# First layer's cross attention as one program instead of a loop of stages

## What is computed

```
xn = layernorm(ctx, ln_x_g, ln_x_b)          # 120 rows of 96
ln = layernorm(x, ln_l_g, ln_l_b)            # 128 rows of 128
q  = ln @ Wq.T
kv = concatenate([xn @ Wkv.T, ln @ Wlkv.T])  # keys: context rows and the rows themselves
k, v = split(kv); split_heads(q, k, v)       # 2 heads of 64
qn = rmsnorm(q) * 64 ** -0.5
kn = rmsnorm(k)
attn = where(mask, qn @ kn.T, -max)          # the mask hides context rows only
out  = softmax(attn) @ v
x = layernorm(x + out @ Wo.T + bo)
```

## Time and profile before

| | us |
|---|---|
| median of 3 runs | 6116.07 |
| the profiled execution | 6122.38 |
| its span, first to last instruction | 6120.6 |
| PE busy in the span | 4768.7 (78%) |
| DVE busy | 4188.5 (68%) |
| ACT busy | 2855.4 (47%) |
| POOL busy | 2427.0 (40%) |
| granted PE clock, mean | 0.877 of 2.4 GHz |

### The profile page before, as it was taken

The page is one execution under the profiler, slowest core; times in us unless marked ns, Lnnn a source line. Parts: engine busy times, 40 slices in busy tenths (PEclk is TensorE's granted clock), DMA queues, the critical chain, the costliest instruction groups (busy, mean ns, idle before and its releaser), DMA issues. The chain is left out here.

```text
span 6120.6 us, 86534 instructions
## 1 busy us (share of the span) xinstructions
PE 4768.7 (78%) x29231; PEld 2856.0 (47%) x29232; DVE 4188.5 (68%) x8013; ACT 2855.4 (47%) x4726; POOL 2427.0 (40%) x2136
## 2 busy tenths in 40 slices
PE   8655999999999999777746676665887689835667
PEld 5543566666666666424522222222664354314444
DVE  3323888888888889576376999997553336547545
ACT  2211677777777777463224554542333325423211
POOL 0011767667677677342174666664001201000100
PEclk9755999999999999887768999998998769966788
DMA  0000000000000000000000000000000000002000
GB/s 14 5 0 30 5 1 20 1 20 1 5 17 1 20 1 5 4 1 2 4 0 7 0 0 0 0 0 12 0 0 13 10 7 7 1 11 58 6 22 7
DMA packets 74599, 49.57 MB, mean 8 GB/s; under 512 B 27801, under 2 KB 68780, under 8 KB 73452
## 3 DMA queue, kind: packets, MB, share of 16 engines
q1 hardware_dynamic: 72171, 43.64, 2.8%
q0 software_dynamic: 2048, 1.05, 0.1%
...
## 5 line engine op out<-in xcount | busy, mean ns | idle before, releaser
L3199 POOL TENSOR_TENSOR l_attn_read<-l_attn_state,l_attn_c_rows 128x1024 f32<-128x1024 f32 x256 | 603.6, 2358 | 329.9 <-DVE l_attn_state L3102 329.0
L2076 POOL TENSOR_TENSOR l_ffn_t<-l_ffn_t 128x512 f32<-128x512 f32 x384 | 488.2, 1271 | 523.1 <-DVE l_ffn_t L1943 523.1
L3102 DVE TENSOR_TENSOR_SCAN l_attn_state<-l_attn_decay,psum 128x1024 f32<-128x1024 f32 x256 | 584.9, 2285 | 8.1
L1676 PE MATMUL psum<-l_ffn_wq,l_ffn_xsT 128*128 128x512 f32 x1152 | 564.9, 599 | 20.8 <-DVE l_ffn_t L1943 12.0
L2904 PE MATMUL psum<-l_attn_read,ident 128*128 128x512 f32 x1024 | 496.9, 608 | 5.4 <-DVE l_attn_yz L3110 3.0
L2895 PE MATMUL psum<-l_attn_parts,pick 96*128 96x512 bf16 x512 | 200.6, 395 | 307.6 <-DVE psum L3094 307.5
L2087 POOL TENSOR_TENSOR l_ffn_p<-l_ffn_p,l_ffn_sm 128x512 f32<-128x512 f32 x384 | 399.2, 1040 | 61.8 <-DVE l_ffn_sm L1975 45.4
L2082 POOL TENSOR_TENSOR l_ffn_t<-l_ffn_t,l_ffn_ss 128x512 f32<-128x512 f32 x384 | 400.4, 1043 | 0.7 <-DVE l_ffn_ss L1958 0.7
L203 POOL TENSOR_SCALAR rstd<-mean_var 128x4 f32<-128x4 f32 (+1 forms) x24 | 5.5, 230 | 979.2 <-DVE mean_var L192 979.2
L3021 ACT COPY l_attn_c_rows<-psum 128x512 f32<-128x512 f32 x256 | 149.6, 584 | 468.4 <-PE psum L2895 468.3
L3094 DVE TENSOR_TENSOR psum<-psum,l_attn_du 128x1024 f32<-128x1024 f32 x256 | 315.6, 1233 | 32.1 <-POOL l_attn_du L3176 4.6
...
## 6 DMA issues: line engine op xcount, KB each, us to landing
...
```

The source lines that it names most:

```text
L1676: nc.tensor.matmul(ring[it % 2], xsT[:, n % 2, m % G, :], wq[:, z, i * 512:(i + 1) * 512], start=True, stop=True).then_inc(itemed, 1)
L2076: nc.gpsimd.tensor_tensor(t1[:, m % G, i, :], t1[:, m % G, i, :], t2[:, x % 3, :], ALU.add).then_inc(added, 1)
L3102: nc.vector.tensor_tensor_scan(state[:, k % 3, :], decay[:, k % 3, :, :, :].rearrange("p h g t -> p (h g t)"), drive, 0.0, ALU.mult, ALU.a ...
L3199: nc.gpsimd.tensor_tensor(read[:, k % 3, :].rearrange("p (h n) -> p h n", h=2), state[:, k % 3, :].rearrange("p (h n) -> p h n", h=2), row ...
```

## The change

`l0_xattn` is written anew; nothing else differs. The loop of stages becomes one `stage` with 48 semaphores and a program written out for six steps `t = 0..5`. In step t the engines work on three groups at once: group `a = t` is normed, projected and scaled (A), group `b_ = t - 1` is attended to (B), and group `f = t - 2` gets its residual and layer norm (F). Step 0 holds only A, step 1 A and B, steps 2 and 3 all three, step 4 B and F, step 5 F.

What is computed in another way:

- The scores are made twice. Once as before, rows of queries (`lat_score`, `ctx_score`), from which DVE takes only the maximum of each query and head. Then turned, rows of keys (`lat_turned`, `ctx_turned`), into which PE first brings minus the maximum, and the mask, by a product with `select` or `select_mask` (two rows in each half of `top_turned`: the maximum, and ones). ACT exponentiates them from PSUM, so the probabilities need no transposition.
- The two heads lie in the two halves of the partitions (`half(z)`), so a product of one head uses 64 rows of the array, or writes 64 of its columns (`value`).
- The sums of the probabilities are products with 64 columns of ones (line 973, 975), which leaves them repeated over the partitions: DVE takes the reciprocal of all 128 x 512 numbers (1156) and multiplies once (1161). The result is already turned for the output projection.
- The output bias is added to the residual on POOL (1201) instead of by PE. POOL also scales the normed context (1182) and the final rows (1190); ACT scales the normed rows of x (1048). All were DVE's.
- The mask's load is issued first, the bias is loaded repeated over 128 partitions.

```diff
--- before.py
+++ after.py
@@ -808,119 +808,397 @@
...
+        bo, x_bias = sb("bo", [128, D]), sb("x_bias", [128, G, D])
...
+        select, select_mask = sb("select", [128, T]), sb("select_mask", [128, NB, NC_])
+        ones64 = sb("ones64", [128, dh])
...
+        half = lambda z: slice(64 * z, 64 * z + 64)
+        A = lambda t: t if t < NG else None
+        B = lambda t: t - 1 if 0 <= t - 1 < NG else None
+        F = lambda t: t - 2 if 0 <= t - 2 < NG else None
+        STEPS = range(NG + 2)
...
+                def qk_turn(g):
+                    for part, m in enumerate(parts):
+                        pe.wait_ge(normed, 3 * g + part + 1)
+                        if g and part == 0:
+                            pe.wait_ge(ctx_exp, H * g)
+                            pe.wait_ge(o_ready, g)
+                        for b in range(G):
+                            last = nc.tensor.transpose(K.bank[4 + part][:, b * m:(b + 1) * m], qkn[:m, part, b * D:(b + 1) * D], K.ident[:m, :m])
...
+                def lat_score(g):
+                    pe.wait_ge(qk_moved, 3 * g + 2)
+                    for b in range(G):
+                        at = slice(b * T, b * T + T)
+                        for z in range(H):
+                            last = nc.tensor.matmul(K.bank[4 + z][:, at], qT[half(z), at], kT[half(z), at], start=True, stop=True)
+                            if b == G - 1:
...
+                    for z in range(H):
+                        nc.tensor.matmul(K.bank[6 + z][:, :KEYS], K.ones[64 * z:64 * z + 1, :], mask_all[64 * z:64 * z + 1, g * G:(g + 1) * G, :], start=True, stop=False,
...
+                def turn_top(g):
+                    pe.wait_ge(top_ready, g + 1)
+                    for b in range(G):
+                        last = nc.tensor.transpose(K.bank[4][:, b * T:(b + 1) * T], top[:, b, :], K.ident[:])
...
+                def lat_turned(g):
+                    pe.wait_ge(top_moved, g + 1)
+                    for z in range(H):
+                        nc.tensor.matmul(K.bank[5 + z], select[half(z), :], top_turned[half(z), :], start=True, stop=False, skip_group_check=True)
+                    for b in range(G):
+                        at = slice(b * T, b * T + T)
+                        for z in range(H):
+                            last = nc.tensor.matmul(K.bank[5 + z][:, at], kT[half(z), at], qT[half(z), at], start=False, stop=True, skip_group_check=True)
+                            if b == G - 1:
+                                last.then_inc(lat_low, 1)
+
...
+                def ctx_turned(g):
+                    for z in range(H):
+                        for b in range(G):
+                            nc.tensor.matmul(K.bank[(7, 4)[z]][:NC_, b * T:b * T + T], select_mask[half(z), g * G + b, :], top_turned[half(z), b * T:b * T + T],
+                                             start=True, stop=False, skip_group_check=True)
+                            last = nc.tensor.matmul(K.bank[(7, 4)[z]][:NC_, b * T:b * T + T], cT[half(z), b * NC_:(b + 1) * NC_], qT[half(z), b * T:b * T + T],
+                                                    start=False, stop=True, skip_group_check=True)
+                        last.then_inc(ctx_low, 1)
...
+                    for z in range(H):
+                        nc.tensor.matmul(K.bank[5][half(z), :], ones64[:], p_lat[:, z, :], start=True, stop=False, skip_group_check=True)
+                    for z in range(H):
+                        last = nc.tensor.matmul(K.bank[5][half(z), :], ones64[:NC_, :], p_ctx[:, z, :], start=False, stop=True, skip_group_check=True)
+                    last.then_inc(summed, 1)
...
+                            nc.tensor.matmul(K.bank[6][half(z), at], v_lat[:, g % 2, b, dh * z:dh * z + dh], p_lat[:, z, at], start=True, stop=False, skip_group_check=True)
...
+                for t in STEPS:
+                    a, b_ = A(t), B(t)
+                    if b_ is not None:
+                        qk_turn(b_)
+                    if a is not None:
+                        in_turn(a, False)
+                    if b_ is not None:
+                        lat_score(b_)
+                    if a is not None:
+                        in_turn(a, True)
+                    if b_ is not None:
+                        ctx_score(b_)
+                    if a is not None:
+                        project(a, 0)
+                        project(a, 1)
+                    if b_ is not None:
+                        turn_top(b_)
+                    if a is not None:
+                        project(a, 2)
+                    if b_ is not None:
+                        lat_turned(b_)
+                    if a is not None:
+                        values_in(a, False)
+                    if b_ is not None:
+                        ctx_turned(b_)
+                    if a is not None:
+                        values_in(a, True)
+                    if b_ is not None:
+                        value(b_)
+                        out(b_)
...
+                const(nc.vector.tensor_tensor(first[:], K.ident[:, 0:1], K.ident[:, 64:65], ALU.add))
+                const(nc.vector.tensor_tensor(second[:], K.ident[:, 1:2], K.ident[:, 65:66], ALU.add))
+                const(nc.vector.tensor_scalar(first[:], first[:], -1.0, None, ALU.mult))
+                const(nc.vector.tensor_scalar(select[:], K.ones[:], first[:], None, ALU.mult))
...
+                        nc.vector.tensor_tensor(K.y[:].rearrange("p g d -> p (g d)"), K.bank[7], x_bias[:].rearrange("p g d -> p (g d)"), ALU.add).then_inc(y_made, 1)
...
+                    if a is not None and a:
+                        stats_of(a)
...
+                        nc.vector.tensor_tensor(top[:].rearrange("p g (z r) -> p g z r", z=H)[:, :, :, 0], top_l[:], top_c[:], ALU.max).then_inc(top_ready, 1)
...
+                            dve.wait_ge(ctx_low, H * b_)
+                        nc.vector.tensor_copy(top_turned[:], K.bank[4]).then_inc(top_moved, 1)
...
+                        dve.wait_ge(summed, 2 * b_ + 1)
+                        nc.vector.reciprocal(inv[:], K.bank[5]).then_inc(recip, 1)
+                        dve.wait_ge(recip, b_ + 1)
+                        dve.wait_ge(summed, 2 * b_ + 2)
+                        if b_:
+                            dve.wait_ge(out_dot, b_)
+                        nc.vector.tensor_tensor(oT[:], K.bank[6], inv[:], ALU.mult).then_inc(o_ready, 1)
...
+                        for i in range(G):
+                            nc.gpsimd.tensor_scalar(cn[:, i, :], K.ctx_all[:, a * G + i, :], rs_x[:NC_, 1, i:i + 1], nb_x[:NC_, 1, i:i + 1], ALU.mult, ALU.add).then_inc(c_normed, 1)
...
+                            ins = nc.gpsimd.tensor_scalar(K.x_all[:, f * G + i, :], K.y[:, i, :], rs[:, i:i + 1], nb[:, i:i + 1], ALU.mult, ALU.add)
...
+                        nc.gpsimd.tensor_tensor(x_bias[:], K.x_all[:, b_ * G:(b_ + 1) * G, :], rows(bo[:], G), ALU.add).then_inc(x_biased, 1)
```

361 lines of the change are left out of this document (261 added, 100 removed).

## The result

| | before | after |
|---|---|---|
| median, us | 6116.15 (4 runs, 6109.86 to 6118.06) | 5966.89 (4 runs, 5963.5 to 5968.24) |
| profiled execution / span | 6122.38 / 6120.6 | 5968.24 / 5966.5 |
| first attention, to its last write | 258.49 | 253.08 |
| the stage | 329.9 | 174.0 |
| all behind it | 5532.2 | 5539.4 |

The ratio is 0.9757 (0.974 to 0.9774): 149.3 us faster between the medians, where 162.1 were forecast. The time lies inside the predicted range, 13 us above the predicted one.

A forecast was written before the change was run, and what follows sets the result against it. The stage was taken as bound by a serial chain. Steps of 28 + 35 + 72 + 22 + 6.5 = 163.5 us, with borders 167.8 instead of 329.9, gave -162.1: 5954.0 us, range 5926 to 6000.

The forecast's parts named there:

- step 0: Stage opening, from first transfer issue through group 0's norms, projections and scaling until L913 may go: 28 us.
- step 4: Step without projections, attention of the last group, counted to its output projection: 22 us.
- last L989 to last write: Step 5, the last group's output 1.1, residual and statistics 2.1, POOL power 1.7 and four rows: 6.5 us.
- the changes: PE empties itself when switching between full and half array, six or seven times a step: 1.3 us in all.
- the tail: End of a step: DVE's reciprocal with the scaling sticks out beyond PE's values by 2.6 us.
- the clock term: PE's clock falls in each gap, returns after some 8 us of mixed products: 40 passes slower, +4.1 us a step.
- the part that I took as zero: Layers behind the stage: same work, their clock may fall otherwise by a few us, counted as zero.
- 1 (the clock never recovers): Rival: half-array products too thin to raise PE's clock in the stage; +44 us, 5998 us; chance 0.09.
- 2 (never falls): Rival: PE's idle gap counts less than thought, clock stays up; -16 us, 5938 us; chance 0.07.
- 3 (pairs don't overlap): Rival: alternating half-array products don't overlap or half wait for loads; +31 to +60 us, about 6000; chance 0.07.
- 4 (the written-out list is fetched too slowly): Rival: late code holds PE at each instruction; at 0.11 us each the kernel takes 6130 us; chance 0.02.
- 5: Rival: A and B run one after the other, projections waiting too; +15 us, 5969; chance 0.74 together with the forecast.

The follow-up runs named there:

- e_sems: Changed kernel with 48 more unused semaphores, so the stage's border clears 96 instead of 48; 5965.08 us (one run).
- e_again: The changed kernel measured once more with no edit; 5960.12 us, ratio 0.973.
- e_early: Changed kernel with each next group's norms (DVE statistics, POOL's and ACT's part) made one step earlier; 5935.69 us, ratio 0.9696.
- e_fill: Changed kernel with 26 useless identity products on PE ahead of its wait before L879 of groups 1 to 3; 5948.44 us, ratio 0.9722.
- e_ctxpairs: Changed kernel with the turned context scores issued with the two heads alternating instead of head by head; 5951.03 us, ratio 0.9721.
- e_copy: Changed kernel with DVE's reciprocal of the sums replaced by a copy, so it computes something else; 5949.54 us, ratio 0.9712.
- e_serial: Changed kernel with PE doing all of group a's turnings and projections before group b's scores, not interleaved; 5985.45 us (one run).
- e_best: e_early plus alternating context heads, group 0's norms ahead of the parameter wait, output projection behind the next group's turnings; 5926.99 us, ratio 0.9674.
- e_all: e_best with next group's statistics and POOL norms earlier still, and DVE's mask conversion after POOL scales its statistics; 5919.86 us, ratio 0.9679.

## Why the prediction was right

**The mechanism.** The stage was priced as a serial chain, whole, at 167.8 us; it took 174.0. Stretch by stretch:

| | predicted | measured |
|---|---|---|
| opening border and step 0, to the first L913 | 1.75 + 28 | 30.2 |
| step 1, to the first L989 | 35 | 34.9 |
| steps 2 and 3 | 36, 36 | 36.96, 35.99 |
| step 4 | 22 | 24.2 |
| last L989 to last write | 6.5 | 8.0 |
| closing border | 2.5 | 3.71 |

Inside step 2: L989 to L879 10.2 predicted, 9.7 measured; the products to L950 some 12 (6.5 + 4.1 and waits) and 13.7; the rest 10.6 and its share of the changes, 11.1; the tail 2.6 and 2.4. The power of 8 columns was interpolated at 1.7 and took 1.67; the reciprocal, extrapolated from 1 and 64 columns to 512, at 3.4 (the two rows give 3.3) and took 3.36. ACT's and POOL's four rows took 1.65. These were among the widest bounds of the prediction, and its values were right.

**Where the sum was lucky.** The terms of step 0 add up to 29.5 and the hand-overs, not to the 28 that the prediction states. The 28 held (28.4 from the first issue at 254.83 to L913 at 283.24) because the second move lay under the first projections: turning and moving took 2.9 us ahead of them (269.09 to 271.94), not 4.2. And the clock term was right in its price (4.1) with a length that was too short; see below.

**What was off, 6.2 us.** Step 4 (+2.2). Its terms leave out the output projection with which a step begins, 8 passes, 1.6 us (391.12 to 392.75), and the wait for the maxima was 1.6 instead of 1. In this step the clock was low twice. The first time was in the sum (35 passes at "4 to 7", taken as 6, and 5.95 measured), the second was not: the products of L950 and L954 took 3.5 us (401.70 to 405.19), in step 2 at 2.4 GHz 1.95. Even so, all from L950 to the end of the values took 11.2 us, against 8.8 + 0.7 + 1.3 in the sum, so the passes there had been priced 1.1 us too high. The windows of the changed kernel in step 4:

```profile
391.40:394.80 3.40, 3.40 (x18) 3.40 (x18) 1.74 (x8) 0.79 (x2) 0.00 (x0) 0.50 0.00 0
394.80:401.70 6.90, 4.33 (x44) 2.86 (x42) 3.58 (x10) 1.14 (x2) 4.67 (x9) 0.99 0.01 2
401.70:405.10 3.40, 3.40 (x20) 2.37 (x21) 0.00 (x0) 0.00 (x0) 0.00 (x0) 0.50 0.00 0
```

The last group (+1.5): the last projection ran at 1.2 GHz, 2.1 us instead of 1.1, and POOL's rows took 0.44 each instead of 0.372. The border (+1.2): I set 2.5 for 48 semaphores without a row to stand on; e_sems gives 0.055 each, and by that 0.84 + 44 x 0.055 = 3.3 of the 3.7 is explained.

**The rest of the difference, 149.3 instead of 162.1.** 6.2 of 12.8 are the stage. 1.8 are the part that I took as zero: -5.4 ahead of the stage and +7.2 behind it. 4.8 are the choice of execution: the profiled one of before lay 6.2 above its median, that of after 1.4. Of the 7.2 us, 5.7 came in one place, whose window stands here for before and for after: the same instructions, 123.20 us at a mean clock of 0.92 and 128.90 at 0.86.

```profile
2881.00:3004.20 123.20, 109.44 (x1379) 84.69 (x1380) 55.33 (x126) 48.41 (x93) 7.12 (x19) 0.92 0.02 5
```

```profile
2718.60:2847.50 128.90, 115.36 (x1377) 89.44 (x1378) 55.43 (x126) 48.60 (x93) 7.15 (x19) 0.86 0.02 5
```

In e_again the same layers took the same 5539.4, in the other kernels up to 12.7 less and 5.5 more; what sets it was not settled.

**The clock.** Predicted: it falls in each gap before L879 and comes back after some 8 us of mixed products (40 passes, 4.1 us). It came back 12.4 us behind L879 in step 2, after some 51 passes by the prediction's count, and 9.5 us behind it in step 3. From L879 to L950 these steps took 13.7 and 12.7 us, step 3 of e_early 8.6 at 2.4 GHz throughout: the low clock cost 5.1 and 4.1 us. That the gap is the cause e_fill and the comparison of all kernels show; the length is not fixed by it, since in e_ctxpairs and e_copy the clock came back 3.1 and 3.4 us behind L879 after the same 7.2 us of wait. The prediction also read from the earlier trace rows that products on half the rows with a drain between don't raise the clock. For the paired ones here that is no rule: at 405.1 it rose among them.

**The rivals.** 1 (the clock never recovers): the steps stood 37, not 46 apart. 2 (never falls): 0.50 for 12.4 us behind L879. 3 (pairs don't overlap): 16 of L954 in 1.06, 32 passes of the values in 1.76. 4 (the written-out list is fetched too slowly): PE's waits are for xn and oT; none of "issue" is above 0.7 us. 5: e_serial. The rule of the Trainium skill that I weighed ("SBUF — State Buffer", "Who interferes with whom") did nothing at the place that I named: L1133 took 0.17 each of four times, and no final row lay beside it. Once, in step 4, POOL's sum of x and bias still ran for 0.09 us beside it by the profile (398.87 to 400.13, L1133 from 400.04) and neither became longer; spans on POOL are rough, so the pair of two SBUF inputs is as good as untested. The same section of the Trainium skill says that DVE's faster two-port modes, which its conversions in SBUF can enter, block GpSimd for their length. e_best shows a pair that agrees with it (0.20 to 1.16 and 1.23), and e_all takes it away.

**The edits that were to cost nothing.** POOL's sum of x and bias took 1.27 us, not 1.04, and lay beside PE's products; the power of 24 columns, 4.19, held DVE 4.7 us a step without holding PE, except in step 0, where PE's 4.1 us before the first L913 wait for it, as the sum had it.
